# Finer pieces with semaphores of their own, in a new order on every engine: RWKV, RG-LRU and mixture of experts on one core

## The chip, the cores and the metric

The kernel runs on one core of one Trainium2 chip. The metric is the device time of one execution in microseconds (us). Five engines take part, each with an instruction queue of its own: TensorE (PE), VectorE (DVE), ScalarE (ACT), GpSimd (POOL) and SyncE (SP, which issues most DMAs).

## What is computed

For 16 sequences of 512 tokens and 256 channels:

```python
xn = layer_norm(x); lx = time_shift(xn)
k, v, r = mix(xn, lx, m) @ w_key, ... @ w_value, ... @ w_recept
x = x + wkv(exp(time_decay), time_first, k, v) * sigmoid(r) @ w_output
xn2 = layer_norm(x); lx2 = time_shift(xn2)
x = x + sigmoid(fr) * (square(relu(fk)) @ f_w_value)
# layer norm, 4-tap causal convolution, gates, a linear recurrence,
# projection, RMS norm, added to x                        (the "recurrence")
# mixture of experts, 8 experts, 2 per token, on the first 1024 tokens, twice
```

`wkv` is a recurrence over time: for each token it divides a decayed sum of values (alpha) by a decayed sum of weights (beta), in a form kept stable by a running maximum (top).

## The kernel before

Sequences are handled one per **turn**, `TURNS` -1 to 16. Turn i computes the time mixing of sequence i, the channel mixing of sequence i-1 and the recurrence of the p-th finished sequence (`REC_TURN` says in which turn; turns 10, 12 and 16 have two). In turns 3 to 8 and 11 to 16 TensorE also works off 46 expert tiles (`PLACES`), whose weights SP loads. Turns 9 and 10 have none. What every engine does and in which order is written out by hand: each engine's block has functions for the stages (`keys`, `sums`, `norm1`, ...) and one function per turn (`turn_0`, `turn_8`, ...) that calls them; turns 5 to 7 share `turn(i)`. An engine takes its instructions strictly in that order. Engines wait for each other on semaphores; the class `Steps` counts the steps of a stage in one semaphore, so a wait for a step also means that all earlier ones of that stage are done.

A sequence passes these stages (lines of the profile):

- `stats_in` on DVE (L2646: four statistics at L2636, four aggregations, three small ones), then on POOL `norm1` (L521: a power at L514, four rows at L518 into `xhat0`) and `keep1` (L531: the rows once more, into `y`). PE transposes them (`transposes_in`, L1780), ACT writes `xn` (`norm_in`, L883).
- `mix` on DVE (L2655 the differences, L2662 six mixed parts for key, value and receptance), then on PE `keys`, `value_columns`, `recept_columns` (L1785), and on ACT the copies out of PSUM (L901, L906, L911).
- `weights_ahead` (L2698: top), `weights_behind` (L2706 the weight of the token itself, in `g`, and L2711, L2713 the decays, in `dec`) on DVE. `g` shares its memory with the mixed receptance, so `weights_behind` waits for `recept_columns` first. ACT takes exponentials (`weight_exp` L915, `decay_exps` L919).
- `sums` (L2718 beta, L2722, L2724 products, L2726 alpha) and `quotient` (L2731 numerator, L2732 denominator) on DVE, `inverse` on ACT (L923, L925), `gated` on DVE (L2737, L2739), `outputs` on PE (L1798).
- `residual_mid` on DVE (L2744 and statistics), `norm2` on POOL, `transposes_mid`, `norm_mid` on ACT, `mix_second` on DVE; then eight `channel_key` (L1791) and `channel_value` (L1868) on PE with `relu_of` (L933) and `square_of` (L937) on ACT between them.
- the recurrence: `third_stats`, `norm3` (POOL), `transposes_rec`, `conv_in` (ACT), `taps`, `split_taps` (DVE), `gate_products` (PE), `gated_input`, `scaled_input` (POOL, L581, L587), `recur` (DVE, L2805), `rec_products`, `sums_of_squares` (ACT), `finish` (DVE), `mean_power` (L514) and `residual` (L597) on POOL.

At the start DVE also evaluates a logarithm (`log_of_sigmoid`, L2616 to L2628), which needs one power from POOL (L511), and routes the tokens (`route_first`, L2823 to L2836: a cast, a comparison and a scan over 2048 elements at L2827). `split_weights` (L2890) prepares the low parts of two weights. In turn 2 POOL scatters the tokens' places (16 indirect DMAs). At the very end POOL picks the experts' rows (`picking`, L631, 16 indirect DMAs), DVE merges them and SP stores the last two sequences. The stages on which the change bears most:

```python
            def mix_first(b):
                dve.wait_ge(ev1.sem, ev1.count(b, "e1"))
                await_step(dve, kvr, b - 1, "r1")
                await_step(dve, wkv, b - 1, "out")
                mix(mix1, b, ((xk, "mix_k"), (xv, "mix_v"), (xr, "mix_r")))
```

## Time and profile before

| | |
|---|---|
| median of 3 runs | 1400.56 us (1400.34 to 1402.72) |
| the profiled execution, its own time | 1401.28 us |
| its span | 1399.5 us |
| mean granted TensorE clock | 0.965 of full |
| busy: PE / PEld / DVE / ACT / POOL | 1239.2 / 1001.2 / 967.0 / 744.9 / 706.2 us |

PE is the matrix multiplications, PEld the weight loads beside them. Busy time is the sum of the instructions' durations. A number after "x" is a count.
### The profile page before, as it was taken

To read this page: it belongs to the slowest core of one execution; us is meant where nothing else is said; L and a number is where in the kernel's file an instruction comes from. 1 tells how busy PE (TensorE), PEld (TensorE's weight loads), DVE (VectorE), ACT (ScalarE), POOL (GpSimd) and SP (SyncE) were. 2 spreads that over 40 slices of the span, in tenths; PEclk is the share of its full clock that TensorE was granted. 3 is DMA by queue.
4 is the path that set the end of the run, shared out by engine and by line. 5 is a ranking of instruction groups with operands and counts; after the bars stand their busy time and mean duration, and the time that the engine had idled before them with its cause. 6 is when DMAs were issued, how large, how long until landed. Compare 5 with 4: busy or idle time off the path is not lost. (4 is left out here: it accounts for less than half of the span.)

```text
span 1399.5 us, 17020 instructions
## 1 busy us (share of the span) xinstructions
PE 1239.2 (89%) x6050; PEld 1001.2 (72%) x6050; DVE 967.0 (69%) x1470; ACT 744.9 (53%) x1138; POOL 706.2 (50%) x536
## 2 busy tenths in 40 slices
PE   2379899999999999999987678988999999999981
PEld 1257668687887878878775566867878688888871
DVE  5777786666967576686588779868687676455335
ACT  1444545374553735555366557646576556373632
POOL 4244564536556262474565756665664662533215
PEclk9789899999999999999999899999999999999996
DMA  5000034324334243343310002332333353443244
GB/s 175 15 16 1 16 98 138 120 97 135 102 133 151 87 142 118 110 149 104 106 45 1 1 1 98 112 104 82 107 90 114 113 169 114 155 135 128 76 143 124
DMA packets 98371, 137.27 MB, mean 98 GB/s; under 512 B 9000, under 2 KB 83752, under 8 KB 98280
## 3 DMA queue, kind: packets, MB, share of 16 engines
q1 hardware_dynamic: 87408, 119.93, 26.5%
q0 software_dynamic: 4256, 10.24, 2.7%
q10 hardware_dynamic: 6624, 6.03, 1.2%
q8 instruction: 48, 0.79, 0.2%
q14 instruction: 35, 0.29, 0.1%
HBM read 119.64 MB, written 16.54 MB: 97 GB/s over the span
## 5 line engine op out<-in xcount | busy, mean ns | idle before, releaser
L514 POOL TENSOR_TENSOR rstd<-varis,half_neg 128x4 f32<-128x4 f32 x64 | 96.2, 1504 | 293.3 <-DVE varis L2651 150.9
L1868 PE MATMUL psum<-fwv,hid 128*128 128x256 f32 x1024 | 240.3, 383 | 2.3 <-ACT hid L937 2.3
L1868 PEld LDWEIGHTS psum<-fwv,hid 128*128 128x128 f32 x1024 | 194.2, 192 | 30.5 <-ACT hid L937 2.7
L1907 PEld LDWEIGHTS psum<-xst,ew 128*128 128x128 f32 x1472 | 176.9, 192 | 18.0 <-ACT xst L1018 5.8
L1907 PE MATMUL psum<-xst,ew 128*128 128x128 f32 x1472 | 180.9, 276 | 5.1 <-ACT xst L1018 3.2
L1915 PE MATMUL psum<-ew,hidt 128*128 128x256 f32 x736 | 167.0, 380 | 2.1 <-ACT hidt L1024 2.1
L1915 PEld LDWEIGHTS psum<-ew,hidt 128*128 128x128 f32 x736 | 139.0, 190 | 25.3 <-issue 3.3
L1780 PE MATMUL psum<-ident,xhat 128*128 128x128 f32 x368 | 53.4, 293 | 83.5 <-POOL xhat L518 82.4
L518 POOL TENSOR_SCALAR xhat<-rows_ring,negmean,rstd 128x256 f32<-128x256 f32 x108 | 118.9, 1114 | 10.6 <-POOL rstd L514 6.6
L1024 ACT ACTIVATE hidt<-psum 128x512 f32<-128x512 f32 x92 | 55.0, 598 | 121.9 <-PE psum L1907 121.6
L622 POOL DMA_INDIRECT xs<-xf_rows,token_of_slot x46 | 57.7, 1255 | 122.5 <-PE psum L1895 101.5
L1780 PEld LDWEIGHTS psum<-ident,xhat 128*128 128x128 f32 x368 | 45.5, 151 | 92.4 <-issue 73.9
L933 ACT ACTIVATE hid<-psum 128x512 f32<-128x512 f32 x128 | 75.0, 596 | 57.7 <-PE psum L1791 43.2
L1791 PE MATMUL psum<-xfk_hi,fwk_hi 128*128 128x512 f32 x256 | 92.3, 441 | 2.4 <-DVE parts L2670 1.2
L883 ACT ACTIVATE xn<-psum,vec 128x512 f32<-128x512 f32 x64 | 46.2, 773 | 76.9 <-PE psum L1780 76.4
L2737 DVE SCALAR_TENSOR_TENSOR timely<-timely 128x1024 f32<-128x1024 f32 x16 | 22.7, 1421 | 91.7 <-ACT timely L925 91.7
L2777 DVE SCALAR_TENSOR_TENSOR space<-space,vec 128x512 f32<-128x512 f32 x90 | 70.7, 852 | 21.8 <-ACT space L954 21.8
L1791 PE MATMUL psum<-parts,fwk_hi 128*128 128x512 f32 x256 | 80.7, 396 | 0.0
L937 ACT ACTIVATE hid<-hid 128x512 f32<-128x512 f32 x128 | 78.4, 628 | 3.4 <-ACT ys L1032 2.0
L1791 PE MATMUL psum<-xfk_hi,fwk_lo 128*128 128x512 f32 x256 | 80.1, 394 | 0.0
L1791 PE MATMUL psum<-parts,gw_hi 128*128 128x512 f32 x256 | 73.7, 410 | 4.5 <-DVE parts L2670 3.3
L1798 PE MATMUL psum<-gwo,space 128*128 128x256 f32 x240 | 58.1, 398 | 17.2 <-DVE space L2805 17.2
(272 smaller groups left out, 2684.2 us busy)
## 6 DMA issues: line engine op xcount, KB each, us to landing
ew<-in_w SPq DMA_DIRECT2D x92, 1024.0 KB, 5.4
rows_ring<-in_x SPq DMA_DIRECT2D x14, 512.0 KB, 4.7
out<-rows_ring SPq DMA_DIRECT2D x14, 512.0 KB, 3.3
ys_rows<-ys ACTq DMA_DIRECT2D x46, 128.0 KB, 4.7
xf_rows<-ew SPq DMA_DIRECT2D x2, 1024.0 KB, 4.4
xf<-in_x SPq DMA_DIRECT2D x2, 512.0 KB, 4.5
space<-in_f_w_key SPq DMA_DIRECT2D x1, 1024.0 KB, 7.4
fwv<-in_f_w_value SPq DMA_DIRECT2D x1, 1024.0 KB, 9.7
```

The lines of the kernel that those rows point to most:

```text
L514: pool.tensor_tensor(dst, src, half_neg[:, 0:src.shape[1]], ALU.pow).then_inc(done, 1)
L518: pool.tensor_scalar(dst[:, c, :], src[:, c, :], negmean[n][:, c:c + 1], rstd[n][:, col0 + c:col0 + c + 1], ALU.add, ALU.mult).then_inc(st ...
L622: pool.indirect_dma_start(out=xs[n % 2][:], out_offset=None, in_=xf_rows, in_offset=bass.IndirectOffsetOnAxis(ap=token_of_slot[:, t:t + 1] ...
L933: nc.scalar.activation(hid[:, j % NHID, :], ring[f"f{j}"], ACT.Relu).then_inc(relu.sem, 1)
L937: nc.scalar.activation(hid[:, j % NHID, :], hid[:, j % NHID, :], ACT.Square).then_inc(sq.sem, 1)
L1780: last = nc.tensor.transpose(bank_t[:, c, k * P:(k + 1) * P], src[:, k, c * P:(c + 1) * P], ident[:])
L1791: last = nc.tensor.matmul(dst, w[a][:, c, m * P:(m + 1) * P], src[b][:, c, :], start=n == 0, stop=n == len(terms) - 1)
L1798: last = nc.tensor.matmul(dst[:, k, :], src[:, c, k * P:(k + 1) * P], w[:, c, :], start=c == 0, stop=c == chunks - 1)
L1868: last = nc.tensor.matmul(rows4[:, k, :], hid[:, j % NHID, k * P:(k + 1) * P], fwv[:, j, :], start=j == 0 and k % 2 == 0, stop=j == FC - 1 ...
L1907: last = nc.tensor.matmul(bank_e[:, j * P:(j + 1) * P], ew1[:, c, at:at + P], xst[:, c, :], start=c == 0, stop=c == DC - 1)
L1915: last = nc.tensor.matmul(bank_e[:, 0:D], hidt[:, j, :], ew2[:, j, :], start=j == 0, stop=j == FC - 1)
L2777: nc.vector.scalar_tensor_tensor(s.cv[:, c, :], s.xc[:, c, j:j + T], col(f"conv{j}", c), s.cv[:, c, :], ALU.mult, ALU.add).then_inc(conv.s ...
```

## The change

Nothing is computed differently; all operations and their sizes stay. The `wkv` and `wkv_act` semaphores are divided into thirteen. `mix_first` becomes `first_differences`, `mixed_key`, `mixed_value`, `mixed_receptance`; `mix_second` becomes five pieces; `weights_behind` becomes `weights_now` and `weights_decayed`; `sums` and `quotient` become six pieces; `residual_mid` gives its statistics to `second_stats`, `finish` its first instruction to `mean_square`. Then the turn functions of DVE, PE, ACT and POOL are written in a new order, in turns 0 to 4 and 8 to 16 throughout; in `turn(i)` (5 to 7) only DVE's. SP's program stays.

```diff
-        wkv = steps("wkv", ["m0", "m1", "q0", "q1", "cap", "z0", "z1", "in", "b0", "b1", "dv", "gv", "a0", "a1",
-                            "num", "den", "gate", "out"], B)
-        wkv_act = steps("wkv_act", ["g", "dec", "ln", "inv"], B)
+        tops = steps("tops", numbered("m", DC), B)
+        weight_now = steps("weight_now", numbered("q", DC) + ["cap"], B)
+        decays_in = steps("decays_in", numbered("z", DC) + ["in"], B)
+        betas = steps("betas", numbered("b", DC), B)
...
+            def first_differences(b):
+                dve.wait_ge(ev1.sem, ev1.count(b, "e1"))
+                await_step(dve, mixture, b - 1, "out")
+                differences(mix1, b)
+
+            def mixed_key(b):
+                await_step(dve, kvr, b - 1, "k1")
+                await_step(dve, mixture, b - 1, "out")
+                dve.wait_ge(mix1.sem, mix1.count(b, "d"))
+                mixed_part(mix1, xk, "mix_k")
...
+            def weights_decayed(b):
+                was = top[:, :, 0:T]
+                dve.wait_ge(mix1.sem, mix1.count(b, "r1"))
+                await_step(dve, mix2, b - 1, "r1")
+                dve.wait_ge(tops.sem, tops.count(b, "m1"))
                 for c in range(DC):
                     nc.vector.scalar_tensor_tensor(dec[:, 0, c, :], was[:, c, :], decay[:, c:c + 1], top[:, c, 1:T + 1],
-                                                   ALU.add, ALU.subtract).then_inc(wkv.sem, 1)
-                nc.vector.tensor_tensor(dec[:, 1], kc[:], top[:, :, 1:T + 1], ALU.subtract).then_inc(wkv.sem, 1)
...
@@ DVE @@
             def turn_first():
+                stats_in(0)
                 dve.wait_ge(vec_made, 3)
                 log_of_sigmoid()
-                stats_in(0)
                 route_first()
-                mix_first(0)
+                first_differences(0)
+                mixed_key(0)
+                mixed_value(0)
+                mixed_receptance(0)
+                split_weights(1, fwk[1], fwk_whole, fwk[0])
                 weights_ahead(0)
+                split_weights(2, gw[1], gw_whole, gw[0])
 
             def turn_0():
-                weights_behind(0)
+                weights_decayed(0)
                 stats_in(1)
-                sums(0)
-                quotient(0)
+                weights_now(0)
+                beta_sums(0)
+                decayed_values(0)
+                denominators(0)
+                weighted_values(0)
+                alpha_sums(0)
+                numerators(0)
                 gated(0)
-                split_weights(1, fwk[1], fwk_whole, fwk[0])
-                split_weights(2, gw[1], gw_whole, gw[0])
+                first_differences(1)
+                mixed_key(1)
+                mixed_value(1)
                 residual_mid(0)
-                mix_first(1)
+                second_stats(0)
+                mixed_receptance(1)
+                weights_ahead(1)
@@ PE @@
             def turn_0():
...
                 outputs(0)
+                keys(1)
+                value_columns(1)
                 freed(zsum, 0, "z")
                 transposes_mid(0)
-                keys(1)
-                value_columns(1)
                 recept_columns(1)
@@ POOL @@
             def turn_16():
-                mean_power(13)
                 residual(13)
-                next_gather(15, "d")
+                next_gather(16, "a")
                 keep3(14)
-                keep2(15)
-                next_gather(16, "a")
                 next_gather(16, "b")
+                norm3(15)
                 mean_power(14)
-                norm3(15)
+                keep3(15)
                 picking(1, 0)
-                keep3(15)
                 picking(1, 1)
```

**The order on DVE at the start.** `la` and `log_a` belong to the logarithm, `stats`, `moments`, `negmean` and `varis` to the statistics of the first sequence, `ew` to the routing. Before:

```order
L2624 SCALAR_TENSOR_TENSOR la<-la 128x2 x6
L2625 SCALAR_TENSOR_TENSOR la<-la 128x2
L2626 TENSOR_SCALAR la<-vec 128x2
L2627 SCALAR_TENSOR_TENSOR log_a<-la 128x2
L2628 TENSOR_SCALAR log_a<-log_a 128x2
L2636 BN_STATS stats<-xf 128x6 x4
L2639 BN_AGGR moments<-stats 128x2 x4
L2641 TENSOR_SCALAR negmean<-moments 128x4
L2643 TENSOR_SCALAR varis<-moments 128x4
L2651 TENSOR_SCALAR varis<-moments 128x4
L2823 CAST ew<-ew 8x2048
```

Now:

```order
L2655 BN_STATS stats<-xf 128x6 x4
L2658 BN_AGGR moments<-stats 128x2 x4
L2660 TENSOR_SCALAR negmean<-moments 128x4
L2662 TENSOR_SCALAR varis<-moments 128x4
L2670 TENSOR_SCALAR varis<-moments 128x4
L2635 SCALAR_TENSOR_TENSOR la<-vec 128x2
L2637 TENSOR_SCALAR la<-la 128x2
L2638 RECIPROCAL la<-la 128x2
L2639 TENSOR_TENSOR la<-la 128x2
L2640 TENSOR_TENSOR la<-la 128x2
L2641 TENSOR_SCALAR la<-la 128x2
L2643 SCALAR_TENSOR_TENSOR la<-la 128x2 x6
```

The statistics stood behind the logarithm and stand ahead of it.

**The order on DVE from the first turn into turn 0.** `timely` holds top, g, key, value and the sums, `dec` the decays, `fwk_lo` and `gw_lo` are the split weights. Before:

```order
L2698 SCALAR_TENSOR_TENSOR timely<-decay,timely 128x512 x2
L2706 SCALAR_TENSOR_TENSOR timely<-timely,vec 128x512 x2
L2709 TENSOR_SCALAR timely<-timely 128x1024
L2711 SCALAR_TENSOR_TENSOR dec<-timely,decay 128x512 x2
L2713 TENSOR_TENSOR dec<-timely 128x1024
L2636 BN_STATS stats<-xf 128x6 x4
L2639 BN_AGGR moments<-stats 128x2 x4
L2641 TENSOR_SCALAR negmean<-moments 128x4
L2643 TENSOR_SCALAR varis<-moments 128x4
L2651 TENSOR_SCALAR varis<-moments 128x4
L2718 SCALAR_TENSOR_TENSOR timely<-dec 128x512 x2
L2722 TENSOR_TENSOR dec<-dec,timely 128x1024
```

Now:

```order
L2740 SCALAR_TENSOR_TENSOR timely<-decay,timely 128x512 x2
L2958 TENSOR_TENSOR gw_lo<-space,gw_hi 128x1024
L2759 SCALAR_TENSOR_TENSOR dec<-timely,decay 128x512 x2
L2762 TENSOR_TENSOR dec<-timely 128x1024
L2655 BN_STATS stats<-xf 128x6 x4
L2658 BN_AGGR moments<-stats 128x2 x4
L2660 TENSOR_SCALAR negmean<-moments 128x4
L2662 TENSOR_SCALAR varis<-moments 128x4
L2670 TENSOR_SCALAR varis<-moments 128x4
L2748 SCALAR_TENSOR_TENSOR timely<-timely,vec 128x512 x2
L2751 TENSOR_SCALAR timely<-timely 128x1024
L2767 SCALAR_TENSOR_TENSOR timely<-dec 128x512 x2
```

The decays (into `dec`) have come ahead of the token's own weight (L2706 before, L2748 now), which moved behind the statistics of the next sequence, and one of the weight splits lies in this stretch.

**The order on POOL from turn 9 into turn 10.** `rstd1`, `xhat1` are of `norm2`, `rstd2` of `norm3`, `rstd0` with `y` of `keep1`, `rms` of `mean_power`, `space<-space` the two products of the recurrence. Before:

```order
L514 TENSOR_TENSOR rstd1<-varis1,half_neg 128x4
L518 TENSOR_SCALAR xhat1<-y,negmean1,rstd1 128x256 x4
L581 TENSOR_TENSOR space<-space 128x1024
L587 TENSOR_TENSOR space<-space 128x1024
L514 TENSOR_TENSOR rms<-msq,half_neg 128x4
L514 TENSOR_TENSOR rstd2<-varis2,half_neg 128x4
L518 TENSOR_SCALAR xhat0<-xf,negmean2,rstd2 128x256 x4
L597 TENSOR_TENSOR xf<-xf,space 128x1024
L554 TENSOR_TENSOR rows_ring<-rows_ring,y 128x1024
L514 TENSOR_TENSOR rstd0<-varis0,half_neg 128x4
L518 TENSOR_SCALAR y<-rows_ring,negmean0,rstd0 128x256 x4
L541 TENSOR_TENSOR rows_ring<-rows_ring,bias 128x1024
```

Now:

```order
L564 TENSOR_TENSOR rows_ring<-rows_ring,y 128x1024
L524 TENSOR_TENSOR rstd1<-varis1,half_neg 128x4
L528 TENSOR_SCALAR xhat1<-y,negmean1,rstd1 128x256 x4
L524 TENSOR_TENSOR rstd0<-varis0,half_neg 128x4
L528 TENSOR_SCALAR y<-rows_ring,negmean0,rstd0 128x256 x4
L551 TENSOR_TENSOR rows_ring<-rows_ring,bias 128x1024
L591 TENSOR_TENSOR space<-space 128x1024
L597 TENSOR_TENSOR space<-space 128x1024
L524 TENSOR_TENSOR rms<-msq,half_neg 128x4
L524 TENSOR_TENSOR rstd2<-varis2,half_neg 128x4
L528 TENSOR_SCALAR xhat0<-xf,negmean2,rstd2 128x256 x4
L524 TENSOR_TENSOR rstd0<-varis0,half_neg 128x4
```

`keep1(10)` (the rows into `y`) stood behind `mean_power(5)`, `norm3(6)` and `residual(5)`; it stands ahead of them and of both products.

## Rows read from the trace of the kernel before

**Rows 1.** The page, part 1: busy time, share, instructions of TensorE.
```profile
PE 1239.2 (89%) x6050; PEld 1001.2 (72%) x6050; DVE 967.0 (69%) x1470; ACT 744.9 (53%) x1138; POOL 706.2 (50%) x536
```

**Rows 2.** Stretches: us; busy us (count) of PE, PEld, DVE, ACT, POOL; PEclk, DMA.
```profile
0.00:92.00 92.00, 35.61 (x96) 19.88 (x97) 60.13 (x103) 27.02 (x33) 34.05 (x45) 0.83 0.24 73
92.00:345.00 253.00, 238.87 (x1144) 192.74 (x1143) 181.37 (x295) 128.67 (x186) 129.85 (x97) 0.97 0.25 81
345.00:672.00 327.00, 322.07 (x1661) 264.18 (x1660) 227.90 (x319) 177.01 (x276) 173.09 (x128) 1.00 0.39 124
672.00:850.00 178.00, 143.32 (x584) 108.44 (x583) 143.03 (x230) 104.91 (x156) 105.66 (x77) 0.93 0.08 24
850.00:1000.00 150.00, 137.11 (x686) 112.32 (x685) 121.47 (x185) 94.90 (x144) 91.11 (x63) 0.99 0.33 108
...
1331.00:1399.50 68.50, 35.02 (x183) 29.21 (x181) 30.35 (x52) 21.78 (x44) 24.80 (x23) 0.83 0.43 136
```

**Rows 3.** Timeline, PE, 0 to 95 us: start, duration, group, [idle before, releaser].
```profile
21.36 1.94 PE L1780 MATMUL psum<-ident,xhat 128*128 128x128 f32 x8 [21.36 <-POOL xhat L518]
...
55.03 1.97 PE L1780 MATMUL psum<-ident,xhat 128*128 128x128 f32 x8 [15.11 <-POOL xhat L518]
62.02 5.26 PE L1798 MATMUL psum<-wo,dec 128*128 128x256 f32 x16 [5.02 <-DVE dec L2739]
77.92 1.94 PE L1780 MATMUL psum<-ident,xhat 128*128 128x128 f32 x8 [10.64 <-POOL xhat L518]
...
90.85 1.03 PE L1791 MATMUL psum<-xfk_hi,fwk_hi 128*128 128x512 f32 x2
```

**Rows 4.** Timeline, DVE (VectorE), 0 to 95 us.
```profile
9.95 1.40 DVE L2636 BATCH_NORM_STATS2 stats<-xf 128x6 f32<-128x256 f32 x4
...
14.81 4.41 DVE L2827 TENSOR_TENSOR_SCAN ew<-ys,ew 8x2048 f32<-8x2048 f32 x1
...
24.91 1.23 DVE L2655 TENSOR_TENSOR dec<-xn 128x1024 f32<-128x1024 f32 x1 [5.16 <-ACT xn L883]
...
39.95 1.41 DVE L2706 SCALAR_TENSOR_TENSOR timely<-timely,vec 128x512 f32<-128x512 f32 x2 [5.02 <-PE psum L1785]
...
59.39 1.23 DVE L2737 SCALAR_TENSOR_TENSOR timely<-timely 128x1024 f32<-128x1024 f32 x1 [2.21 <-ACT timely L925]
...
61.79 2.28 DVE L2890 TENSOR_TENSOR fwk_lo<-space,fwk_hi 128x2048 fp32r<-128x2048 f32 x1
...
84.81 1.23 DVE L2670 TENSOR_TENSOR parts<-dec,xfk_hi 128x1024 fp32r<-128x1024 f32 x1
```

**Rows 5.** Timeline, POOL (GpSimd), 0 to 95 us.
```profile
15.05 6.17 POOL L518 TENSOR_SCALAR xhat<-xf,negmean,rstd 128x256 f32<-128x256 f32 x4 [0.22 <-POOL rstd L514]
...
22.52 2.17 POOL L518 TENSOR_SCALAR y<-xf,negmean,rstd 128x256 f32<-128x256 f32 x4 [0.21 <-POOL rstd L514]
```

**Rows 6.** Tile xf, 0 to 60 us: landing of the loads of x.
```profile
DMA to landing us min/median/max: 4.1/4.5/4.9
```

**Rows 7.** Timeline, PE, turn 2.
```profile
164.16 1.93 PE L1780 MATMUL psum<-ident,xhat 128*128 128x128 f32 x8 [4.31 <-POOL xhat L518]
```

**Rows 8.** Timeline, PE, turn 10.
```profile
792.79 1.94 PE L1780 MATMUL psum<-ident,xhat 128*128 128x128 f32 x8 [9.62 <-POOL xhat L518]
...
824.51 1.94 PE L1780 MATMUL psum<-ident,xhat 128*128 128x128 f32 x8 [6.63 <-POOL xhat L518]
```

**Rows 9.** Timeline, POOL, turn 9 to 10.
```profile
763.15 1.01 POOL L514 TENSOR_TENSOR rms<-msq,half_neg 128x4 f32<-128x4 f32 x1 [9.86 <-DVE msq L2811]
```

**Rows 10.** Timeline, DVE, turn 10.
```profile
780.79 1.41 DVE L2636 BATCH_NORM_STATS2 stats<-rows_ring 128x6 f32<-128x256 f32 x4 [1.61 <-POOL y L518]
```

**Rows 11.** Timeline, POOL, the end.
```profile
1366.51 1.06 POOL L631 DMA_INDIRECT ew<-ys_rows,slot_i  x1 [24.97 <-DMA ys_rows<-ys]
...
1379.03 2.36 POOL L574 TENSOR_TENSOR rows_ring<-rows_ring,bias 128x1024 f32<-128x1024 f32 x1
```

**Rows 12.** Waits of all engines: us in total, times, longest us.
```profile
DVE timely L2737 <- ACT timely L925: 91.7, 16, 11.5
```

1671 lines of the change are left out of this document (948 added, 723 removed).

## The prediction

> **What bounds the kernel now.** I read the page's first part, then the busy time by stretches, then the timelines of the stretches in which TensorE (PE) waits. The page [rows 1] shows PE busy for 1239.2 of 1399.5 us, so 160.3 us are idle, and VectorE (DVE), ScalarE (ACT) and GpSimd (POOL) have far more room. The stretches [rows 2] show where the idle time lies (length less PE's busy time): 56.4 us before 92 us, 14.1 from there to 345, 4.9 from 345 to 672, 34.7 from 672 to 850 (turns 8 to 10, at the end of the first round of expert tiles), 12.9 from 850 to 1000, 33.5 after 1331; the stretch 1000 to 1331 holds the rest, 3.8. The granted clock is 0.83 at both ends and 0.93 in turns 8 to 10. So a new order can win at four places, and elsewhere it can only lose. Almost everywhere PE waits for the same thing: a normalised tile that POOL has just scaled [rows 3, 7, 8].
>
> **The start.** Step one, the statistics. Now they start at 9.95 us [rows 4], behind the logarithm; x is the first load issued, and it lands 4.9 us after its issue at the latest [rows 6], so some 5.8 us from the span's start. They start 4.1 us earlier. POOL then scales four rows. Before, this took 6.17 us, beside a DVE scan of 4.41 us; the next four rows, beside an idle DVE, took 2.17 [rows 4, 5]. Ahead of the routing they take the 2.17, another 4.0 us. PE's first transposes come at 21.36 - 4.1 - 4.0 = 13.3 us [rows 3].
> The rule that fits is in the Trainium skill, SBUF — State Buffer, "Who interferes with whom": a DVE instruction with two SBUF inputs (or in a two-port mode) and a GpSimd instruction that reads SBUF exclude each other for the whole instruction. Here the trace agrees: 6.17 - 2.17 = 4.0 us is nearly the whole scan.
> The 8.1 us do not all arrive. The mixing waited for xn until 24.91, after 5.16 us idle [rows 4]: DVE was done with the routing at 19.75. Logarithm, statistics and routing only change places, so mixing now starts at 19.7: 5.2 us earlier. Should the last POOL row be caught by the routing after all, it costs up to 4 us of the 6 us between 13.3 and 19.7, thus nothing.
> Step two, the chain to the first projection. DVE waited 5.02 us for the receptance matmuls before it began on weights and decays [rows 4]; now the decays come first and do not wait. Next late is ACT: its exponential of the decays is queued behind the receptance copies, a scaling of wo and a table load. Of the 5.02 us I take 2.3. The denominator is computed before alpha, so that ACT inverts it beside the alpha scans: the 2.21 us wait at L2737 [rows 4] goes. Outputs(0) starts at 62.02 - 5.2 - 2.3 - 2.2 = 52.3 us [rows 3]. The first weight split (2.28 us [rows 4]) and the smaller second leave the stretch behind the gating; there DVE waited for PE anyway, so this is worth nothing; the pieces of the next mix that take their place lie beside outputs(0), 5.26 us [rows 3].
> Step three. PE waited 10.64 us for the transposes at 77.92, and did keys, values and receptances behind them, until 90.85 [rows 3]. Keys and values come ahead now, two thirds of 90.85 - 77.92 - 1.94 = 11.0 us, inside the wait. What ends last is then DVE's second mix: before, its low part ended at 84.81 + 1.23 = 86.0 [rows 4], 8.1 us behind the start of the transposes. New: transposes at 77.92 - 9.7 = 68.2, the first channel_key at 76.3 instead of 90.85, **-14.5 us**. Bounds: -5.2 if only step one holds; -17.4 if DVE could use all 8.1 us.
>
> **Turns 1 to 4.** Of 14.1 us idle the largest wait is 4.31 at 164.16 [rows 7], for sequence 3's tile. Its statistics now come before the sums, and PE has one channel_key and one channel_value more to do first; this wait goes, and the transposes after it (1.93 us against 1.94 at 1.2 GHz elsewhere) are probably no longer cold. On POOL keep2(2) moves between the scatter and norm2(2), one addition more ahead of transposes that PE waits for. I take **-6 us**; bounds -14 (all idle) and +5 (two additions of 2.36 us, the size of the one in [rows 11], fully exposed).
>
> **Turns 5 to 7.** 4.9 us of idle in 327 [rows 2], only DVE's order changes: 0.
>
> **Turns 8 to 10.** Two waits stand out, 9.62 and 6.63 us [rows 8]. The first comes from a queue: POOL stood 9.86 us at mean_power(5) [rows 9], with keep1(10) behind it; DVE's stats_in(11) waited for keep1's y [rows 10], and only then could norm1(11) start. keep1(10) is now ahead of mean_power(5), and stats_in(11) ahead of the sums: this wait goes almost whole, with the cold transposes -10. Next late are the finish of recurrence 5 and the tanh that frees the bank, which I leave 2 us as part of what remains. The 6.63 us are outputs(10), addition, statistics, POOL, transposes in a row; PE gets about as much to do in between as before: -2. The rest, 34.7 - 9.6 - 6.6 = 18.5 us, lies in nine pieces or more and is reached by the same means (recurrence ahead of the late time mixing, values and receptances of turn 9 pulled forward): half, -9. **-21 us**; bounds -40 (all idle and 5 us of clock) and 0.
>
> **Turns 11 to 13.** 12.9 us idle [rows 2], the same kind of order, less room because expert tiles return: a third, **-4 us**; bounds -12 and +6.
>
> **Turns 14 to 16** are full of PE work (3.8 us idle up to 1331), 0. **The end:** PE's last tile, then 16 indirect DMAs that POOL issues one after another from 1366.51, with keep3(15), 2.36 us, in their midst [rows 11]. It now stands in front, where POOL idled 24.97 us: **-2.4 us**, since the last picks end the program.
>
> The added waits (DVE gets one or two more at each piece) are for things long done in most cases; DVE has 432 us of idle time, so I cost them at 0. If DVE were late at a piece, all behind it in its queue would be too.
>
> **Sum:** -14.5 - 6 - 21 - 4 - 2.4 = -47.9 us. Against the profiled execution, 1401.28: 1353.4; the median of the runs is 0.7 lower, so **1352.7**.
>
> **Rivals.**
> (A) *The middle gives nothing.* Each wait moved in turns 1 to 4 and 8 to 13 comes back at the next place. For it: waits for POOL's tiles stand everywhere [rows 3, 7, 8], and chain length, not order, may hold turns 9 and 10, where PE has no tiles to fill with. Against: rows 9 and 10 show a pure queueing loss. -16.9: 1383.7.
> (B) *Slower: DVE shuts POOL out.* The new order fills DVE's pauses with two-input work. A tile scaled beside such work took 6.17 instead of 2.17 us [rows 5], 4 us more. Turns 8 to 16 hold 27 such tiles (8 + 8 + 11) on the way to transposes. PE then waits at L1780. From 12 tiles on that are each 4 us later, and not already so before, the gain of 48 is used up; with 15 it is 12 us slower, 1412.6. Against: many of the tiles are slow already. The rule of the SBUF page above speaks for this rival; it names the exclusion for every two-input instruction.
> (C) *The first turn's statistics do not lead.* x lands later, or the logarithm's power on POOL, which is queued ahead of norm1(0), is late. The start keeps steps two and part of three: 9 us less gain, 1361.7.
> (D) *The order fits better than I grant:* three quarters of the idle time in turns 8 to 13 goes. (34.7 + 12.9) x 0.75 = 36 instead of 25, 1341.7.
> In-order waiting on ACT (gated has waited for the inverse 16 times, 91.7 us in all [rows 12], largely hidden from PE) is part of A.
>
> **Chances.** Forecast 0.53, A 0.16, B 0.10, C 0.07, D 0.11, no change within 0.2% (2.8 us, what a measurement of this kernel can tell) 0.03. So faster 0.87, same 0.03, slower 0.10. The range 1338 to 1385 takes in A, C and D and leaves out B and the case of no change.
>
> **What would show it.** Start: first transposes near 13 us, mixing near 19.7, outputs(0) near 52, first channel_key near 76; idle before 92 us down to some 42 (an A-like start would have it above 50). Turn 10: the wait before transposes_in(11) under 3 us and POOL's wait at L514 for msq without keep1 behind it. Turns 8 to 10: idle near 15 instead of 35. The end: 16 picks without an addition between. Wrong would be: L518 tiles in the changed kernel clearly slower on average with PE waiting on them (B), or the same waits under other names between 672 and 1000 (A).

## The result and the profile after

The changed kernel takes 1346.28 us (median of 4 runs, 1343.87 to 1348.99), the kernel before in the same series 1400.97 us: a ratio of 0.9601, with a 95% interval of 0.9583 to 0.9619. That is 54.7 us faster; 1352.7 were predicted (47.9 faster), with a range of 1338 to 1385. The profiled execution took 1348.99 us, the slowest of the four, 2.7 above the median; its span is 1347.3 us, 52.2 less than before. Of all executions in this document one slow one, of `new_to_turn_0`, at 2617.53 us, is left out of the ratios.

Against [rows 1], the page of after, part 1: PE is busy for almost as long as before, so what went is idle time, 48.9 of the 52.2 us. ACT has 8 instructions more and 8.6 us more busy time. They are table loads (97 with 125.7 us against 89 with 115.3), so "all operations stay" holds but for these: the new order on ACT changes its table more often.

```profile
PE 1235.9 (92%) x6050; PEld 1002.1 (74%) x6050; DVE 946.0 (70%) x1470; ACT 753.5 (56%) x1146; POOL 693.7 (51%) x536
```

The windows of both kernels, cut where PE begins the same work: the first channel_key; transposes_rec(1), with which turn 5 begins (358.44, now 334.56); the value projection of sequence 8 (603.15, now 579.24); the transposes of sequence 12's tile (882.53, now 837.02); the last transposes (1344.23, now 1294.43); the end. The columns are those of [rows 2]. First before, then after.

```profile
0.00:90.85 90.85, 34.46 (x93) 19.10 (x93) 59.58 (x102) 26.47 (x32) 34.05 (x45) 0.83 0.24 74
90.85:358.44 267.59, 253.46 (x1204) 201.43 (x1203) 195.24 (x308) 133.68 (x194) 142.44 (x106) 0.97 0.26 84
358.44:603.15 244.71, 239.78 (x1248) 200.09 (x1247) 168.11 (x244) 130.79 (x207) 118.07 (x92) 1.00 0.38 121
603.15:882.53 279.38, 242.25 (x1085) 189.18 (x1084) 219.63 (x345) 169.60 (x251) 166.23 (x115) 0.96 0.19 59
882.53:1344.23 461.70, 445.79 (x2314) 372.12 (x2313) 299.12 (x438) 266.46 (x423) 224.84 (x163) 0.99 0.37 118
1344.23:1399.50 55.27, 23.52 (x116) 19.28 (x114) 25.37 (x36) 17.91 (x32) 20.59 (x17) 0.79 0.41 128
```

```profile
0.00:79.23 79.23, 37.63 (x92) 20.52 (x93) 61.36 (x105) 26.96 (x33) 34.23 (x45) 0.83 0.27 84
79.23:334.56 255.33, 249.31 (x1202) 200.32 (x1203) 188.07 (x306) 135.16 (x195) 133.83 (x103) 0.98 0.27 85
334.56:579.24 244.68, 239.75 (x1249) 200.08 (x1248) 167.63 (x245) 130.82 (x207) 124.23 (x95) 1.00 0.39 125
579.24:837.02 257.78, 238.06 (x1068) 185.19 (x1066) 216.44 (x342) 165.55 (x248) 161.76 (x116) 0.97 0.20 64
837.02:1294.43 457.41, 446.43 (x2332) 375.86 (x2331) 289.04 (x442) 277.17 (x433) 221.06 (x164) 0.99 0.37 120
1294.43:1347.30 52.87, 24.73 (x114) 20.17 (x114) 23.42 (x36) 17.87 (x32) 18.57 (x17) 0.76 0.43 134
```

| stretch | before | after | moved | predicted |
|---|---|---|---|---|
| to the first channel_key | 90.85 | 79.23 | -11.6 | -14.5 |
| turns 1 to 4 | 267.59 | 255.33 | -12.3 | -6 |
| turns 5 to 7 | 244.71 | 244.68 | 0.0 | 0 |
| turns 8 to 10 | 279.38 | 257.78 | -21.6 | -21 |
| turns 11 to 16, up to the last transposes | 461.70 | 457.41 | -4.3 | -4 |
| the end | 55.27 | 52.87 | -2.4 | -2.4 |

One border does not cut quite the same work. Part of an expert tile, 16 matmuls `psum<-xst,ew`, stands ahead of sequence 12's transposes before (at 880.75 us) and behind them now (at 837.93). From its start to the next row is 1.8 us. With that put right, turns 8 to 10 gave 19.8 us and the stretch behind them 6.1.

The places. The start, PE (as in [rows 3]), DVE ([rows 4]) and POOL ([rows 5]), in this order; the last line is a row of before that [rows 5] does not have, the tile of norm2(0).

```profile
12.12 1.94 PE L1798 MATMUL psum<-ident,xhat 128*128 128x128 f32 x8 [12.12 <-POOL xhat L528]
23.01 6.22 PE L1803 MATMUL psum<-timely,wk 128*128 128x512 f32 x8 [8.95 <-DVE timely L2675]
...
52.83 6.67 PE L1816 MATMUL psum<-wo,dec 128*128 128x256 f32 x16 [8.69 <-DVE dec L2803]
...
71.01 1.94 PE L1798 MATMUL psum<-ident,xhat 128*128 128x128 f32 x8 [4.64 <-POOL xhat L528]
...
79.23 0.70 PE L1809 MATMUL psum<-xfk_hi,fwk_hi 128*128 128x512 f32 x2 [1.30 <-issue]
```

```profile
5.23 1.41 DVE L2655 BATCH_NORM_STATS2 stats<-xf 128x6 f32<-128x256 f32 x4 [4.20 <-DMA xf<-in_x]
...
20.11 1.20 DVE L2687 TENSOR_TENSOR dec<-xn 128x1024 f32<-128x1024 f32 x1
```

```profile
9.75 2.22 POOL L528 TENSOR_SCALAR xhat<-xf,negmean,rstd 128x256 f32<-128x256 f32 x4 [0.22 <-POOL rstd L524]
...
65.05 5.81 POOL L528 TENSOR_SCALAR xhat<-y,negmean,rstd 128x256 f32<-128x256 f32 x4 [0.21 <-POOL rstd L524]
```

```profile
73.27 4.50 POOL L518 TENSOR_SCALAR xhat<-y,negmean,rstd 128x256 f32<-128x256 f32 x4 [0.21 <-POOL rstd L514]
```

The statistics lead (5.23 us), POOL's first tile takes 2.22 instead of 6.17 us, and PE's first transposes come at 12.12 instead of 21.36 us. But norm2(0)'s rows take 5.81 us, and outputs(0) takes 6.67 us where it took 5.26.

PE in turn 2 (against [rows 7]) and turn 10 (against [rows 8]):

```profile
171.62 1.94 PE L1798 MATMUL psum<-ident,xhat 128*128 128x128 f32 x8 [4.03 <-POOL xhat L528]
```

```profile
755.92 1.10 PE L1798 MATMUL psum<-ident,xhat 128*128 128x128 f32 x8 [1.11 <-ACT sf L952]
...
780.60 1.06 PE L1798 MATMUL psum<-ident,xhat 128*128 128x128 f32 x8 [1.41 <-POOL xhat L528]
```

The 9.62 us wait before transposes_in(11) has become 1.11 and the 6.63 before transposes_mid(10) 1.41 us. A wait of 4.03 us stands in turn 2 again, now before transposes_mid(2). POOL at the end (against [rows 11]) has keep3(15) in front of the picks:

```profile
1292.66 2.35 POOL L584 TENSOR_TENSOR rows_ring<-rows_ring,bias 128x1024 f32<-128x1024 f32 x1
1316.70 1.07 POOL L641 DMA_INDIRECT ew<-ys_rows,slot_i  x1 [21.69 <-DMA ys_rows<-ys]
```

And PE's largest wait in sum, with times and the longest; before, it was 82.4 us in 15 waits:

```profile
PE psum L1798 <- POOL xhat L528: 38.4, 9, 12.1
```

### The profile page after: what moved, and what is told of

The parts are those of the page before. It is cut to its first block and busy times, and to the rows that moved or that the text cites. A ratio compares the mean times of both kernels' runs of the same rounds, so it can differ in the third digit from the quotient of the medians.

```text
span 1347.3 us, 17198 instructions
## 1 busy us (share of the span) xinstructions
PE 1235.9 (92%) x6050; PEld 1002.1 (74%) x6050; DVE 946.0 (70%) x1470; ACT 753.5 (56%) x1146; POOL 693.7 (51%) x536
## 5 line engine op out<-in xcount | busy, mean ns | idle before, releaser
L1886 PE MATMUL psum<-fwv,hid 128*128 128x256 f32 x1024 | 237.0, 380 | 0.4 <-ACT hid L947 0.4
L524 POOL TENSOR_TENSOR rstd<-varis,half_neg 128x4 f32<-128x4 f32 x64 | 89.9, 1404 | 226.6 <-DVE varis L2662 120.3
L632 POOL DMA_INDIRECT xs<-xf_rows,token_of_slot x46 | 62.3, 1355 | 106.7 <-PE psum L1913 92.6
L2843 DVE SCALAR_TENSOR_TENSOR space<-space,vec 128x512 f32<-128x512 f32 x90 | 65.1, 790 | 39.7 <-ACT space L964 39.7
L1042 ACT ACTIVATE ys<-psum 128x256 f32<-128x256 f32 x46 | 17.6, 382 | 113.7 <-PE psum L1933 113.6
L2675 DVE SCALAR_TENSOR_TENSOR timely<-dec,vec,xn 128x512 f32<-128x512 f32 x96 | 76.7, 858 | 1.8
```

The source lines that it names most:

```text
L524: pool.tensor_tensor(dst, src, half_neg[:, 0:src.shape[1]], ALU.pow).then_inc(done, 1)
L632: pool.indirect_dma_start(out=xs[n % 2][:], out_offset=None, in_=xf_rows, in_offset=bass.IndirectOffsetOnAxis(ap=token_of_slot[:, t:t + 1] ...
L1886: last = nc.tensor.matmul(rows4[:, k, :], hid[:, j % NHID, k * P:(k + 1) * P], fwv[:, j, :], start=j == 0 and k % 2 == 0, stop=j == FC - 1 ...
L2675: nc.vector.scalar_tensor_tensor(dst[:, c, :], diff[:, c, :], col(m, c), xn[:, c, 0:T], ALU.mult, ALU.add).then_inc(st.sem, 1)
L2843: nc.vector.scalar_tensor_tensor(s.cv[:, c, :], s.xc[:, c, j:j + T], col(f"conv{j}", c), s.cv[:, c, :], ALU.mult, ALU.add).then_inc(conv.s ...
```

## The experiments

Twelve kernels ran (one of them the changed kernel again), in four series of runs on four chips, each series with the kernel before beside it (1409 to 1411 us there, against 1401 in the first series). So kernels of different series are compared by their ratio to before and by their places in the trace. There is one trace of each kernel, and only the first series has one of the kernel before.

### Pieces and order, one without the other

`pieces_old_order` has the changed kernel's functions and semaphores, and the calls of the kernel before:

```diff
-                stats_in(0)
                 dve.wait_ge(vec_made, 3)
                 log_of_sigmoid()
+                stats_in(0)
...
-                keep3(15)
                 picking(1, 0)
+                keep3(15)
                 picking(1, 1)
```

> The divided semaphores and pieces of the changed kernel, but every engine's instructions in the order of the kernel before; only the waits differ. Theory (all of the gain is order, the added waits are for things long done): 1401 us, between 1399 and 1403. Rival (the finer semaphores themselves release somebody earlier, or the added waits cost): more than 3 us away from 1401 on either side.

Measured: 1402.47 us, ratio 0.9949 (0.9930 to 0.9968). The time is the theory's, but the kernel before took 1410.37 beside it, so on this chip the pieces alone are worth 7.9 us, 0.5%. That is what the rival says, that finer semaphores release somebody earlier; only its mark, 3 us from 1401, was set for a chip on which before takes 1401.

Where? The span (1399.4 us) is that of the trace of before (1399.5), which was taken on another chip. A better partner is the trace of `stats_first_alone` below: same chip, and the kernel before in all but the place of the first statistics. From outputs(0) to the end it takes 1345.5 us, the pieces 1337.2. From outputs(1) to outputs(2) the pieces take 57.0 us against 60.1 (60.8 in the trace of before), from outputs(8) to outputs(9) 75.4 against 80.7 (80.7 too); every other such step differs by at most 1.7 us. In the second stretch PE has 2.0 us less idle and 3.3 us less busy time, at a granted clock of 1.00 instead of 0.96. Which of the divided semaphores does it was not tested. So "all of the gain is order" does not hold on these chips: some 8 us of it are the pieces'. For the first series the share is not known.

`new_to_turn_4` takes the new order up to turn 4 and the old one from turn 5; `new_from_turn_5` is the reverse. At that border all engines have had the same calls in both orders.

> New order on all engines from the start to turn 4, the order of before from turn 5 to the end. Theory (start and turns 1 to 4 give 23.9 us, and later turns pass it on, since in turns 5 to 7 both kernels have under 6 us idle): 1377 us (1374 to 1380), the first channel_key at 79.2 us from the span's start, the values of sequence 8 24 us earlier than in the kernel before. Rival A for this half (later waits take it back, since chains and not PE's work set turns 9 and 10): 1385 or more.

> The order of before up to turn 4, the new order from turn 5 to the end. Theory (the two parts add up: the profiles stand 52.2 us apart, 23.9 of them before turn 8): 28.3 us faster, 1373 us (1370 to 1377), of which 2.4 lie in the last picks. Idle time of PE in turns 8 to 10 near 18 us instead of 35. Rival (the middle needs the lead that the start gained): 1385 or more.

Measured: 1376.50 us, ratio 0.9759 (0.9743 to 0.9775), and 1372.70 us, ratio 0.9735 (0.9719 to 0.9751). Both lie within the times expected, but before is 10 us slower on this chip than the one they were reckoned from. Against the pieces alone it is -26.0 and -29.8 us, -55.7 in sum. In the second kernel turns 8 to 10 take 257.7 us with 19.7 us of idle time (18 expected), as in the changed kernel (257.8 and 19.7), without the lead from the start. The changed kernel once more:

> The changed kernel once more, unchanged, as the partner of the runs beside it. Theory (the parts of the order add up: the two half-orders took 26.0 and 29.8 us off the kernel with the pieces alone, 1402.5): 55.8 us less than that, 1346 to 1347 us if this is the same chip. Rival (the halves share a gain): 1352 or more.

Measured: 1345.28 us, ratio 0.9543 (0.9527 to 0.9559), 57.2 below the pieces alone. The two halves add up, and turns 5 to 7, full of PE work, hand a lead on whole: 244.71 and 244.68 us in the two kernels. Rival A is out for both halves. (This was another chip; before took 1410.72 us there, so the change is worth 65 us on it, 8 of them the pieces', against 54.7 in the first series. The changed kernel differs by 1 us between them.)

### The start

`new_to_turn_0` takes the new order up to turn 0 alone.

> New order up to turn 0, the order of before from turn 1. Theory (the start and turns 1 to 4 are two separate gains): first channel_key at 79 to 80 us as in the changed kernel, and 11 to 12 us less than the kernel with the pieces alone at the end, about 0.987 of before. Rival (turn 2 takes it back: with the statistics alone moved, a lead of 4.6 us at the transposes of turn 2 was gone 30 us later, behind the 16 scatters on POOL): the lead is over 10 us until turn 2 and under 6 us from there to the end, 0.991 or more of before.

Measured: 1386.48 us, ratio 0.9815 (0.9796 to 0.9835). Below the pieces alone this is 18.9 us by the ratios, 16.0 by the medians and 12.4 by the spans (1387.0 in the slowest of the three executions counted, against 1399.4); 11 to 12 and about 0.987 were expected. The start was not that of the changed kernel, either. The first channel_key comes at 73.86 us, not at 79 to 80: weights_ahead(1) and the routing product come later on DVE here, and POOL's rows of norm2(0) are quick:

```profile
63.80 2.17 POOL L528 TENSOR_SCALAR xhat<-y,negmean,rstd 128x256 f32<-128x256 f32 x4 [0.21 <-POOL rstd L524]
```

In the traces the lead is 14.4 us at outputs(1), 15.4 at outputs(2), and 12.5 from outputs(4) to the last transposes; the rival's loss in turn 2 is out for all but 3 us of it. The start is a gain of its own. Turns 1 to 4 are worth another 11.9 us by the spans (1375.1) and 7.9 by the ratios.

`stats_first_alone`, an edit of the kernel before:

```diff
+                stats_in(0)
                 dve.wait_ge(vec_made, 3)
                 log_of_sigmoid()
-                stats_in(0)
```

> The kernel before with one edit: the statistics of the first sequence ahead of the logarithm on VectorE. Theory (step one of the prediction, 5.2 us, all of it passed on): first transposes at 12 to 13 us, mixing at 19.7 to 20.1, first channel_key at 85.7, 1396 us. Rival 1 (the edit alone gains nothing, since keep1(0)'s rows and the decays are what comes next): first channel_key above 89 us, 1399 to 1401. Rival 2 (the earlier start only moves a later wait): first channel_key at 86 but 1399 or more at the end.

Measured: 1405.53 us, ratio 0.9964 (0.9950 to 0.9978), 4.8 us less than before beside it. Timelines of DVE and PE:

```profile
19.71 1.20 DVE L2655 TENSOR_TENSOR dec<-xn 128x1024 f32<-128x1024 f32 x1
```

```profile
22.62 6.58 PE L1785 MATMUL psum<-timely,wk 128*128 128x512 f32 x8 [2.54 <-DVE timely L2662]
...
58.17 5.89 PE L1798 MATMUL psum<-wo,dec 128*128 128x256 f32 x16 [5.02 <-DVE dec L2739]
...
76.43 5.22 PE L1785 MATMUL psum<-timely,wk 128*128 128x512 f32 x8
...
87.95 1.03 PE L1791 MATMUL psum<-xfk_hi,fwk_hi 128*128 128x512 f32 x2
```

Mixing starts at 19.71 us, 5.2 earlier as predicted, but the first channel_key at 87.95, only 2.9 earlier than in the trace of before: between the theory (85.7) and rival 1 (above 89). The missing 2.3 us lie in three PE rows: keys(0) took 6.58 instead of 5.32, outputs(0) 5.89 instead of 5.26 [rows 3], keys(1) 5.22 instead of 4.90 us. The same 8 matmuls of a projection take 3.60 us elsewhere. All three rows come soon after a pause of PE, and got more of the lower clock than before. The granted clock is 0.62 during outputs(0) and 0.69 during keys(1), against 0.70 and 0.73 before. For keys(0) the view shows 1.00 in both traces, since the profile's record of the clock starts only there: its first entry, the full clock, stands at 28.5 us (31.1 before), 5.9 us after keys(0) began (3.4 before). At half the clock until then the rows lose half of that, 3.0 and 1.7 us, which is what they took beyond 3.60.

`quiet_rows`, an edit of the changed kernel:

```diff
                 mixed_value(1)
+                mixed_receptance(1)
                 residual_mid(0)
                 second_stats(0)
-                mixed_receptance(1)
-                weights_ahead(1)
...
-                route_second()
                 second_differences(0)
                 channel_mix_key(0)
                 channel_mix_high(0)
                 channel_mix_low(0)
                 channel_mix_receptance(0)
+                weights_ahead(1)
                 weights_decayed(1)
                 weights_now(1)
+                route_second()
                 stats_in(2)
```

> The changed kernel, with VectorE kept still while POOL scales the rows that the first transposes_mid waits for (5.81 us in the changed kernel, beside two scans and the routing product): the mixed receptance comes ahead of residual_mid(0), into 2.65 us of idle time; weights_ahead(1) and route_second come behind the second mix. Theory (what stretches these rows is work of VectorE beside them, as 6.17 against 2.17 us at the start): rows 2.2 us, transposes_mid(0) 3.6 us earlier, at 67.4 us, first channel_key near 75.6, the whole 3 to 4 us faster than the changed kernel. Rival 1 (the stretch has another cause, the rows stay above 4 us): no gain. Rival 2 (the late scans of sequence 1 take it back by outputs(1)): first channel_key at 75.6 but less than 1 us at the end.

Measured: 1349.37 us, ratio 0.9561 (0.9540 to 0.9583): no gain. POOL:

```profile
63.38 2.16 POOL L528 TENSOR_SCALAR xhat<-y,negmean,rstd 128x256 f32<-128x256 f32 x4 [0.21 <-POOL rstd L524]
...
88.69 9.12 POOL L528 TENSOR_SCALAR xhat<-rows_ring,negmean,rstd 128x256 f32<-128x256 f32 x4 [0.20 <-issue]
```

The rows took 2.16 instead of 5.81 us, so what stretches them is VectorE's work beside them: that part of the theory holds. Two more traces agree, 2.17 us in `new_to_turn_0` and, below, 4.11 in `undo_two`, where only the routing product stands beside them. Transposes_mid(0) came at 65.69 and the first channel_key at 73.41 us (71.01 and 79.23 in the first trace of the changed kernel, 68.92 and 77.14 in the one of this series). Rival 2 took the rest. The scans and the routing now stand ahead of stats_in(2); sequence 2's tile (88.69, 9.12 us) came no earlier than in the changed kernel (88.77), PE waited 2.33 us for it, and at transposes_mid(1) 0.2 us of lead were left against the first trace, none against the other.

`undo_two` undoes two moves of the changed kernel, at the start (with norm_mid(0) on ACT and weights_ahead(1) on DVE, not shown) and at the end:

```diff
                 outputs(0)
-                keys(1)
-                value_columns(1)
                 freed(zsum, 0, "z")
                 transposes_mid(0)
+                keys(1)
+                value_columns(1)
                 recept_columns(1)
...
-                keep3(15)
                 picking(1, 0)
+                keep3(15)
                 picking(1, 1)
```

> The changed kernel with two of its moves undone, far apart, each read at its place. (1) Start: keys(1) and value_columns(1) behind transposes_mid(0) again on TensorE, norm_mid(0) ahead of keys_out(1) on ScalarE, weights_ahead(1) behind the second mix. Theory (step three of the prediction, that the projections lie inside the wait, is worth some 5 us): transposes_mid(0) where it was or a little earlier, first channel_key 5 to 7 us later than in the changed kernel, at 83 to 86 us. Rival (the second mix is what ends last anyway): at most 1.5 us later. (2) The end: keep3(15) between the picks again. Theory: 2.4 us from the end of the last tile to the end of the span. Rival: hidden behind the landing of the picks, under 0.5 us. Together 6 to 9 us slower than the changed kernel if turns 1 to 4 pass the first on, 0.959 to 0.961 of before.

Measured: 1349.82 us, ratio 0.9572 (0.9558 to 0.9587), 4.5 us above the changed kernel of the series before. PE:

```profile
68.38 1.94 PE L1798 MATMUL psum<-ident,xhat 128*128 128x128 f32 x8 [9.79 <-POOL xhat L528]
...
80.65 1.03 PE L1809 MATMUL psum<-xfk_hi,fwk_hi 128*128 128x512 f32 x2
```

The first channel_key comes 1.4 us later than in the first trace of the changed kernel, 3.5 later than in the second (77.14); 5 to 7 were expected, at most 1.5 by the rival. But with weights_ahead(1) out of the way the transposes themselves came earlier. From transposes to channel_key it is 12.3 us again, where the changed kernel needs 8.2: step three is worth 4.1 us there. From outputs(2) to outputs(8) the kernel is 4.0 to 4.2 us behind the changed one's second trace, from outputs(9) on 5.0. From the first pick to the end of the span it is 32.95 us, against 30.6 in the changed kernel and 33.0 before: keep3(15) is worth the 2.4 us.

### Turn 10

Is the 9.62 us wait a queue, as the prediction says? Two edits of the kernel with the pieces alone, both with stats_in(11) ahead of finish(5) on DVE. `keep1_ahead`, POOL in turn 9:

```diff
                 norm2(9)
+                keep2(9)
+                keep1(10)
                 gated_input(5)
                 scaled_input(5)
                 mean_power(5)
                 norm3(6)
                 residual(5)
-                keep2(9)
-                keep1(10)
```

> Old order with the divided pieces and one queue mended: on POOL keep2(9) and keep1(10) go ahead of the recurrence steps of sequence 5 (gated_input, scaled_input, mean_power), on VectorE stats_in(11) goes ahead of finish(5). Theory (the 9.62 us wait in front of transposes_in(11), 7.09 in the kernel with the pieces alone, is queueing): that wait falls under 2 us and the whole is 5 to 8 us faster than the kernel with the pieces alone (0.9949 of before), so 0.989 to 0.992 of before. Rival (the chain behind it is the limit, outputs(10) to transposes_mid(10)): the wait moves to transposes_mid(10), 6.56 us before, now 10 or more, and the whole gains under 2 us.

Measured: 1403.70 us, ratio 0.9947 (0.9926 to 0.9967), no gain over the 0.9949 of the pieces. PE, then DVE:

```profile
763.00 5.66 PE L1808 MATMUL psum<-gwo,space 128*128 128x256 f32 x16 [10.14 <-DVE space L2862]
...
790.90 1.09 PE L1790 MATMUL psum<-ident,xhat 128*128 128x128 f32 x8 [0.56 <-ACT sf L952]
```

```profile
760.51 2.34 DVE L2862 TENSOR_TENSOR_SCAN space<-space 128x512 f32<-128x512 f32 x2 [8.29 <-POOL space L597]
```

The wait at 790.90 fell to 0.56 us, but PE stood 10.14 us before rec_products(5). The two steps of POOL ahead of gated_input(5) and scaled_input(5) made recur(5) wait 8.29 us, and the second mix of sequence 9 is queued behind it on DVE. The rival had named another place, with the same sum. `keep1_in_gap` puts keep2(9) and keep1(10) between scaled_input(5) and mean_power(5):

> The queue of turn 9 mended a second way, on the kernel with the pieces alone: on POOL keep2(9) and keep1(10) go only ahead of mean_power(5), into the 10 us in which POOL stands there, and no longer ahead of gated_input(5) and scaled_input(5), which last time held up recur(5) by 8.29 us; stats_in(11) stays ahead of finish(5). Theory (the wait before transposes_in(11) is queueing, and the recurrence is not touched): rec_products(5) keeps its wait of about 2 us, the wait before transposes_in(11) falls from 7.09 to under 1.5 us, and the whole is 5 to 8 us faster than with the pieces alone (0.989 to 0.992 of before). Rival (the chain of outputs(10) and transposes_mid(10) is the limit of turn 10): the 6.6 us there grow by what is won, and the whole gains under 2 us (0.993 or more).

Measured: 1398.20 us, ratio 0.9923 (0.9908 to 0.9938). POOL, then PE:

```profile
757.11 7.06 POOL L528 TENSOR_SCALAR y<-rows_ring,negmean,rstd 128x256 f32<-128x256 f32 x4 [0.21 <-POOL rstd L524]
...
777.01 5.70 POOL L528 TENSOR_SCALAR xhat<-rows_ring,negmean,rstd 128x256 f32<-128x256 f32 x4 [0.30 <-POOL rstd L524]
```

```profile
757.35 5.32 PE L1808 MATMUL psum<-gwo,space 128*128 128x256 f32 x16 [3.98 <-DVE space L2862]
...
821.17 1.09 PE L1790 MATMUL psum<-ident,xhat 128*128 128x128 f32 x8 [3.16 <-POOL xhat L528]
```

keep1's rows fill POOL's pause and more (7.06 us, beside DVE's work), and norm1(11) starts at 777.01 instead of 784.46 us. The wait before transposes_in(11) is gone altogether (it was 7.09 us) and that before transposes_mid(10) fell from 6.56 to 3.16, but rec_products(5) waits 3.98 instead of 1.92, and 2.04 and 3.32 us stand before outputs(10) and transposes_rec(7). The theory's "the recurrence is not touched" did not hold: keep2(9) now runs beside the scans of recur(5), which took 4.39 us (2.34 in the pieces alone). From turn 11 on the kernel is 3.8 to 4.1 us ahead of the pieces alone, half of what was expected. The queue is real; this step moved by itself gets half of its wait. The change, which also moves the recurrence and the late mixing, gets some 20 us in turns 8 to 10; which of these moves brings the rest was not tested.

### Beyond the change

`routing_in_pauses`: of the routing only the cast and the comparison stay ahead of the mixing, and

```diff
                 second_stats(0)
-                mixed_receptance(1)
                 weights_ahead(1)
+                dve.wait_ge(hat2.sem, hat2.count(0, f"h{TC - 1}"))
+                route_scan()
...
                 scatter_tokens()
-                keep2(2)
                 norm2(2)
+                keep2(2)
                 norm_power(0)
```

> The changed kernel taken further. VectorE: of the routing only the cast and the comparison stay at the start (xn is there at 15.6 us, the mixing began at 20.1); its scan goes behind weights_ahead(1) and waits until POOL has scaled the rows of norm2(0); route_second goes into the pause behind mixed_receptance(2), and mixed_receptance(1) into that ahead of residual_mid(0). TensorE's routing_products follow channel_key(0, 2). POOL: norm2(2) ahead of keep2(2) in turn 2. Theory: mixing at 15.7 us (4.4 earlier), rows of norm2(0) 2.2 instead of 5.8 us, first channel_key at 70 to 73 us instead of 77 to 79; turn 2's transposes_mid another 2.3 us; the whole 6 to 9 us faster than the changed kernel, 1337 to 1340 us, about 0.949 of before. Rival 1 (the quiet rows alone had won 5 us at the first channel_key and lost all of it by turn 2): under 2 us at the end. Rival 2 (the scan after the rows holds up the second mix): first channel_key after 74 us.

Measured: 1346.29 us, ratio 0.9549 (0.9532 to 0.9567), no gain over the changed kernel. PE:

```profile
19.11 5.53 PE L1803 MATMUL psum<-timely,wk 128*128 128x512 f32 x8 [4.71 <-DVE timely L2675]
...
72.79 1.19 PE L1809 MATMUL psum<-xfk_hi,fwk_hi 128*128 128x512 f32 x2 [4.95 <-issue]
...
177.75 0.70 PE L1809 MATMUL psum<-xfk_hi,fwk_hi 128*128 128x512 f32 x2 [3.07 <-issue]
```

keys(0) starts at 19.11 instead of 23.01 us, but the scan holds up the second mix, the first channel_key waits 4.95 us, and from there to the transposes of sequence 2 PE takes 23.0 instead of 20.5 us, at a granted clock of 0.90 instead of 1.00. In turn 2 the transposes_mid come 4.2 us earlier than in the changed kernel's second trace, and channel_key(2, 0) then waits 3.07. On DVE the experts' norm stands ahead of the second mix, and it needs norm_power(0), which started at 168.59 us, only 1.1 earlier than in that trace (169.68); the lead ends there.

`scatter_divided` moves the experts' rows behind the second mix and divides the scatters, on the unchanged start:

```diff
-                scatter_tokens()
-                keep2(2)
+                scatter_tokens(range(NCH - 1))
                 norm2(2)
+                scatter_tokens(range(NCH - 1, NCH))
                 norm_power(0)
+                keep2(2)
...
-                experts_rows(0)
                 second_differences(2)
                 channel_mix_key(2)
                 channel_mix_high(2)
                 channel_mix_low(2)
+                experts_rows(0)
```

> The changed kernel with turn 2 mended alone, its start untouched. POOL: 14 of the 16 scatters, then norm2(2), then the other two, norm_power(0), and keep2(2) last; VectorE: the experts' rows behind the second mix of sequence 2. In the changed kernel the statistics of norm2(2) were ready at 162.5 us, the scatters ended at 164.7 and keep2(2) at 167.1. Theory (transposes_mid(2) waits 4.0 us for a place in POOL's queue, and turns 3 to 7, with under 6 us idle, pass a lead on): the 4.0 us wait under 1 us, transposes and values behind it warm (1.7 us), the second mix no longer behind the experts' norm, so 4 to 6 us less from turn 3 on, about 1340 us or 0.951 of before. Rival 1 (the second mix or the gathers become the wait: DVE's gated_values(1) began late in several runs of this stretch): lead under 1.5 us at turn 3. Rival 2 (the scatters' landing holds up the first expert tile): PE waits before tile_in(0).

Measured: 1342.31 us (1342.04 to 1343.63), ratio 0.9521 (0.9508 to 0.9534). PE:

```profile
166.91 1.04 PE L1799 MATMUL psum<-ident,xhat 128*128 128x128 f32 x8
...
176.56 0.71 PE L1810 MATMUL psum<-xfk_hi,fwk_hi 128*128 128x512 f32 x2 [1.17 <-issue]
...
190.57 0.44 PE L1914 MATMUL psum<-ident,xs 128*128 128x128 f32 x2 [1.63 <-DMA xs<-xf_rows,token_of_slot]
```

From the transposes of sequence 3 to turn 8 it is 436.3 us instead of 438.2 to 438.4 in the two traces of the changed kernel: 2.1 us, half of the least expected. Its median is the lowest of all kernels here. That it beats the changed kernel is not shown: the intervals (0.9508 to 0.9534, 0.9527 to 0.9559) overlap, and they are from different chips.

## Why the prediction was right, point by point

**The sum.** 47.9 us were predicted, 52.2 came in the profiled execution and 54.7 between the medians. The forecast case was the right one. Between the borders of the table four of six terms were met within 0.6 us; with the border put right, turns 8 to 10 are 1.2 us under their term and the stretch behind them 2.1 over it. The start and turns 1 to 4 missed by more, 2.9 and 6.3 us, in opposite directions: that the sum came so near is in part luck. Part of the gain may also be the pieces', which the prediction costed at 0: on another chip they alone brought 7.9 us.

**Step one** held: statistics at 5.23 us (5.8 foretold), four rows in 2.22 us (2.17), transposes at 12.12 (13.3), mixing at 20.11 (19.7). Rival C, that the statistics do not lead, is out. What the step left out is the clock: alone, the edit moved mixing by 5.2 us and the first channel_key by 2.9 against the trace of before.

**Step two** held: no wait at gated, outputs(0) at 52.83 us (52.3).

**Step three** was mis-sized, -11.6 instead of -14.5 for the start as a whole. "Transposes at 77.92 - 9.7 = 68.2" took the durations between outputs(0) and the transposes from before. They came at 71.01: 0.5 us from the start of outputs(0), 1.4 since it took 6.67 instead of 5.26 us, 1.3 since norm2(0)'s rows took 5.81 instead of 4.50, less 0.5 for a shorter power. Behind them it is 8.2 us to the channel_key, 8.1 foretold. Counted by idle and busy time: PE's idle time before the first channel_key fell from 56.4 to 41.6 us, where "some 42" was foretold (before 92 us), and the same work took 3.2 us more busy time (34.46 to 37.63), where no change was. The rows are slow because the new order puts two scans and the routing product beside them, as `quiet_rows` shows (2.16 us without all three). One by one the four rows took 2.11, 2.65, 0.55 and 0.55 us: the first ended at 67.16, behind the second scan (66.87), the second at 69.79, behind the product (69.35). Rows 5 had shown the price of such company, and the prediction used it only for the first tile.
By the Trainium skill, SBUF — State Buffer, "Who interferes with whom", of two such instructions the one that issues first holds the shared ports to its end, and the other waits. The trace agrees here too, with the ends of the first two rows.

**Turns 1 to 4** gave 12.3 us instead of 6, a term mis-sized by half. Idle time fell by 8.1 us (14.1 to 6.0), near the 6 taken. The other 4.2 are PE's busy time for the same work, so the clock, which the term held at nothing ("probably no longer cold" for one set of transposes only). The windows from outputs(1) to outputs(2), 220 instructions in each, before and after:

```profile
115.34:176.11 60.77, 55.04 (x220) 0.89 0.03 9
```

```profile
103.40:155.40 52.00, 50.53 (x220) 0.93 0.05 11
```

4.5 us of busy time, at a granted clock of 0.89 and 0.93. The widest difference between rows is in the receptances. Before, they stand behind the routing's 32 small matmuls, which took 5.65 us at a granted clock of 0.65, and take 6.76 us at 0.56; now they stand ahead of them (first row before, second after; part of this is paid back in the channel_key rows behind, at 0.66):

```profile
137.51 6.76 PE L1785 MATMUL psum<-timely,wr 128*128 128x512 f32 x8
```

```profile
119.78 3.60 PE L1803 MATMUL psum<-timely,wr 128*128 128x512 f32 x8
```

The bound of +5 for the additions on POOL had its reason too: the 4.03 us wait in turn 2 is scatters and keep2(2) ahead of norm2(2), and `scatter_divided` removes it.

**Turns 5 to 7**: 0 foretold, 0.0 found. **Turns 8 to 10**: -21 foretold, -21.6 found, -19.8 for the same work; the wait before transposes_in(11) is 1.11 us (under 3 foretold), and the one before transposes_mid(10) fell by 5.2 us, where 2 were foretold. Idle time is 19.7 us (37.1 before, in a somewhat wider stretch than that of [rows 2]), not "near 15". And the reason given for its size was too simple: moving keep1(10) and stats_in(11) was to bring about 10 us, and the same move by itself brings 0 or 4, depending on where keep1(10) goes. "Next late are the finish of recurrence 5 and the tanh" should have been recur(5) itself, with the second mix queued behind it. **The end**: -2.4 exactly.

**Rival B**, DVE shutting POOL out, did not come. The tiles of norm2, before and after, by line and form:

```profile
L518 POOL TENSOR_SCALAR xhat<-y,negmean,rstd 128x256 f32<-128x256 f32 x64 | 62.7, 990 | 3.6 <-issue 3.4 <-POOL rstd L514 0.2
```

```profile
L528 POOL TENSOR_SCALAR xhat<-y,negmean,rstd 128x256 f32<-128x256 f32 x64 | 47.4, 755 | 3.3 <-issue 3.0 <-POOL rstd L524 0.2
```

They are faster, 755 instead of 990 ns each; `y`, which nobody on PE waits for, is slower (1099 instead of 1046). So the exclusion decides single places, as in step three, and not the whole. Rival A is out by the two half-orders. D did not come: from the values of sequence 8 to the last transposes, a wider stretch than D names, idle time fell from 53.0 to 30.7 us, by two fifths, not by three quarters.

## What to carry to other kernels

Price a removed wait twice: the idle time, and the clock that PE has lost for the work behind it (2.3 us lost beside 5.2 won with the statistics alone, 4.2 more won beside 8.1 in turns 1 to 4). When a step is moved to where its engine is idle, ask first what else feeds from that queue: the same keep1(10), with keep2(9), was worth 0 in front of the recurrence's inputs and 4 us behind them. And keep VectorE's two-input work off the stretch in which POOL scales a tile that PE waits for, but only if what you push back is not the next chain: the quiet rows won 5 us (3 against the trace of their own series) and lost them within one turn.
